# A three-part decoder layer on one core: prologue put in another order, first gate and up products ahead of the last head outputs, one bias product for two of three value blocks

## The reference, cut to what matters

```python
x = x + attn(layernorm(x))            # scores[0, -1] = scores[-1, 0] = -1e9, softmax over keys
x = x + xattn(layernorm(x), ctx, ctx, mask)
                                      # softmax(axis=1): over the 16 heads; V = ctx @ Wv + bv
x = x + ffn(layernorm(x))             # silu(gate) * up, then down
# ffn: inputs and weights in blocks of 16, block scales rounded to e4m3, values to the FP4 grid
```

## Time and profile before

| | |
|---|---|
| median of 3 runs | 611.21 us (610.62 to 612.62) |
| the profiled execution, its own time | 611.0 us |
| its span in the trace | 609.3 us |
| PE busy | 534.1 us, 88% |
| DVE busy | 511.8 us, 84% |
| ACT busy | 333.7 us, 55% |
| POOL busy | 354.6 us, 58% |
| mean granted TensorE clock | 0.975 of full |

### The profile page before, as it was taken

The page is one execution under the profiler, slowest core; times in us unless marked ns, Lnnn a source line. Parts: engine busy times, 40 slices in busy tenths (PEclk is TensorE's granted clock), DMA queues, the critical chain, the costliest instruction groups (busy, mean ns, idle before and its releaser), DMA issues. The chain is left out here.

```text
span 609.3 us, 14913 instructions
## 1 busy us (share of the span) xinstructions
PE 534.1 (88%) x6171; PEld 383.7 (63%) x6182; DVE 511.8 (84%) x658; ACT 333.7 (55%) x569; POOL 354.6 (58%) x292
## 2 busy tenths in 40 slices
PE   6799999997879999999999999998999676777855
PEld 6677777776557777767676667766776542443433
DVE  3687888897769878888898888888799989899997
ACT  3566766765445655555655575557555544444522
POOL 6411463333226677668768978877789764555540
PEclk9899999999989999999999999999999897899989
DMA  8910000000110011110110011101100000000001
GB/s 192 311 55 2 2 2 3 2 2 1 39 36 2 13 34 45 45 24 25 45 46 19 28 45 46 42 6 44 45 9 6 5 9 9 0 19 17 19 18 52
DMA packets 16645, 20.78 MB, mean 34 GB/s; under 512 B 2821, under 2 KB 14322, under 8 KB 16578
## 3 DMA queue, kind: packets, MB, share of 16 engines
q1 hardware_dynamic: 14658, 19.04, 10.5%
q10 hardware_dynamic: 1920, 0.79, 0.6%
HBM read 16.16 MB, written 1.84 MB: 30 GB/s over the span
## 5 line engine op out<-in xcount | busy, mean ns | idle before, releaser
L446 POOL TENSOR_TENSOR work<-work,rden 125x1792 f32<-125x1792 f32 x48 | 172.2, 3587 | 3.8
L985 ACT ACTIVATE work<-scores 125x896 f32<-125x896 f32 x96 | 88.7, 981 | 95.9 <-PE scores L1360 94.5
L707 DVE TENSOR_REDUCE negmax<-scores 125x112 bf16<-125x1792 f32 x48 | 97.2, 2025 | 26.8 <-PE scores L1350 26.0
L715 DVE TENSOR_REDUCE den<-work 125x56 f32<-125x896 f32 x96 | 102.1, 1064 | 12.3 <-ACT work L985 11.9
L444 POOL TENSOR_TENSOR rden<-rden,stays 125x112 f32<-125x112 f32 x48 | 22.0, 458 | 81.1 <-DVE rden L720 81.0
L1360 PE MATMUL scores<-negmax,identb 125*125 125x448 bf16 x192 | 47.4, 370 | 16.5 <-DVE negmax L707 13.8
L620 DVE TENSOR_REDUCE a_mpad<-scores 112x8 bf16<-112x896 f32 x32 | 33.5, 1093 | 22.1 <-PE scores L1252 20.6
L1350 PE MATMUL scores<-qz,kT 32*125 32x224 f32 x768 | 49.8, 373 | 1.8 <-ACT work L985 1.1
L1386 PE MATMUL head_out<-work,v 125*32 125x112 f32 x1536 | 48.9, 267 | 0.2 <-POOL work L446 0.2
L1457 PE MATMUL wide<-ctxT,ck 128*128 128x375 f32 x128 | 48.2, 498 | 0.8 <-ACT ctxT L1005 0.8
L1468 PE MATMUL wide<-cv,ctxT 128*125 128x256 f32 x192 | 48.5, 378 | 0.0
(11 more groups left out here) (238 smaller groups left out, 1182.1 us busy)
## 6 DMA issues: line engine op xcount, KB each, us to landing
ctx_sb<-in_ctx SPq DMA_DIRECT2D x16, 375.0 KB
mask_sb<-in_mask_Bx1xSxS_if SPq DMA_DIRECT2D x16, 164.1 KB, 5.6
xsx<-in_x SPq DMA_DIRECT2D x4, 448.0 KB, 9.2
out_x<-ores SPq DMA_DIRECT2D x6, 256.0 KB, 2.1
a_raw_w<-in_L_ffn_gate_w SPq DMA_DIRECT2D x1, 1024.0 KB, 6.0
a_raw_w<-in_L_ffn_up_w SPq DMA_DIRECT2D x1, 1024.0 KB, 8.5
a_raw_w<-in_L_ffn_down_w SPq DMA_DIRECT2D x1, 1024.0 KB, 11.9
xt<-xsx SPq DMA_DIRECT2D x4, 112.0 KB, 2.2
```

The source lines that it names most:

```text
L446: pool.tensor_tensor(ex2[0:KP, kc], ex2[0:KP, kc], over, ALU.mult).then_inc(s["prob"], 1)
L707: dve.tensor_reduce(negmax[0:KP, :], scores[0:KP, :, 0:4 * TOK].rearrange("p j (h t) -> p t j h", h=4), AX.XY, ALU.max, negate=True).then_ ...
L715: link(dve.tensor_reduce(den[0:KP, kc, half], ex2[0:KP, kc, :, half, :].rearrange("p g t s -> p t g s"), AX.XY, ALU.add))
L985: act.activation(ex2[0:KP, kc, 4 * i:4 * i + 4].rearrange("p (j m) t s -> p j m s t", m=NE), scores[0:KP, 2 * i:2 * i + 2, 0:4 * TOK].rear ...
```

## The change

- **Loads.** SP issues the value weights second, and waits for the fourth attention weight (not the biases) before the feed-forward weights, each with a semaphore of its own. ACT issues the biases before the output weights, and also the bias `cbv`.
- **Tables.** POOL's twenty-two affine selects go; DVE makes the tables from the identity matrix in eight instructions (`mask_tables`).
- **First tiles.** The first three sequences are written out on PE, ACT and DVE: the rows of scores of sequence 0 come before the projections of sequence 1. The output weights are transposed into bank `head_out` and not `scores`. Statistics of group 1 come before the first row maxima, those of groups 2 and 3 behind them, each followed by its `shift`.
- **Value bias.** It moves from POOL at t = 8 to DVE at t = 2.
- **Passage to cross-attention.** On PE `score_rows` stands before the context input, `query` behind `maxima_T`, half of the first key product behind `maxima_T`. ACT normalises sequence 0 one iteration sooner and copies the context before the weight magnitude. In n = 0 PE subtracts the maximum after one value block instead of two, and DVE adds the last residual before the second block's maximum.
- **Passage to feed-forward.** On PE `gate(0, 0)` and `up(0, 0)` stand before the last sequence's head outputs of block 0, `gate(0, 1)` before the projection, `up(0, 1)` and `x_T(1)` before the head outputs of block 1. DVE takes the joint block maximum of x right behind the first `hidden`.
- **Bias product.** Blocks 0 and 1 of the values share a PSUM bank; one product of 512 columns (the 256 read twice) stands for two of 256.

```diff
@@ -317,19 +327,19 @@
...
-                sp.dma_start(raw[:, 0], whole(a_wq)).then_inc(ld_w[0], 16)
+                for n, w in ((0, a_wq), (2, a_wv)):
+                    sp.dma_start(raw[:, n], whole(w)).then_inc(ld_w[n], 16)
...
-                sp.wait_ge(ld_b, 48)
+                sp.wait_ge(ld_w[3], 16)
...
-                    if t == WFIRST + 2:
-                        value_bias()
...
@@ -586,7 +556,25 @@
...
+                def mask_tables():
+
+
+                    dve.wait_ge(a_s["made"], 2)
+                    link(dve.tensor_reduce(e_rows[:], identb[:].rearrange("p (j r) -> p r j", r=32)[:, 0:3, :], AX.X, ALU.add))
+                    link(dve.tensor_copy(aux[:], e_rows[:, 2:3].to_broadcast([P, TOK])))
...
@@ -604,6 +592,19 @@
...
+                def value_bias():
+
+                    dve.wait_ge(ld_v, 16)
+                    rest = cbv
+                    for n in range(3):
+                        link(dve.tensor_copy(bv_part[:], rest[:]))
+                        last = dve.tensor_copy(bv_parts[32 * n:32 * n + 1, :], bv_part[32 * n:32 * n + 1, :])
+                        if n < 2:
+                            link(last)
+                            link(dve.tensor_tensor(bv_rest[:], rest[:], bv_part[:], ALU.subtract))
+                            rest = bv_rest
+                    last.then_inc(s["bv_parts"], 1)
...
@@ -774,19 +775,24 @@
...
+                def joined_block_max(p):
                     if p == 0:
                         dve.wait_ge(s["wide_read"], 3 * B)
+                    b_amax = next(scale_parts(p))
+                    dve.wait_ge(s["x_norm"], 2 * joined[p] + 2)
+                    dve.tensor_reduce(b_amax[:, HBK:HBK + XBK], blocks(x_unit[:]), AX.X, ALU.max, apply_absolute_value=True)
...
@@ -860,17 +866,21 @@
...
-                for t in range(B + LAG):
+                statistics(1)
+                shift(1)
+                for t in range(1, B + LAG):
                     b = t - LAG
-                    if 0 <= b < B:
-                        row_max(b, 0)
-                        row_max(b, 1)
+                    if t != 2:
+                        row_max(rows_of(t), 0)
+                        row_max(rows_of(t), 1)
                     if 0 <= b - 1:
                         outputs(b - 1)
-                    if t < 3:
-                        statistics(t + 1)
-                    if 1 <= t < 4:
-                        shift(t)
+                    if t == 1:
+                        for g in (2, 3):
+                            statistics(g)
+                            shift(g)
+                    if t == 2:
+                        value_bias()
...
@@ -903,9 +913,10 @@
...
                         head_sum(now, 0, 0)
-                        key_max(now, 1)
                     if n == 0:
                         a_residual(B - 1)
+                    if now:
+                        key_max(now, 1)
...
@@ -933,6 +944,7 @@
...
                 hidden(0, 0)
+                joined_block_max(0)
                 residual(in_turn(B - 2))
                 hidden(0, 1)
...
-                for n, w in ((1, a_wk), (2, a_wv), (3, a_wo)):
-                    act.dma_start(raw[:, n], whole(w)).then_inc(ld_w[n], 16)
+                act.dma_start(raw[:, 1], whole(a_wk)).then_inc(ld_w[1], 16)
                 with nc.allow_non_contiguous_dma(reason="biases, one value per partition"):
                     for dst, bias in ((abq, a_bq), (abk, a_bk), (abv, a_bv)):
                         act.dma_start(dst[:], bias.rearrange("(a p) -> p a", p=P)).then_inc(ld_b, 16)
+                act.dma_start(raw[:, 3], whole(a_wo)).then_inc(ld_w[3], 16)
+                act.dma_start(cbv[:], c_bv.unsqueeze(0).to_broadcast([KP, D])).then_inc(ld_v, 16)
...
@@ -1099,62 +1112,87 @@
...
+                a_input_copy(0)
+                a_normal(1)
+                act.wait_ge(ld_b, 48)
+                act.wait_ge(a_s["bv_cols"], 1)
+                a_queries_keys(0)
+                a_values(0)
+                weight_copy(3, woT)
+                a_input_copy(1)
+                a_normal(2)
+                maxima_copy(0)
+                a_queries_keys(1)
+                a_values(1)
+                a_input_copy(2)
+                a_exp(0)
+                a_queries_keys(2)
+                a_values(2)
+                act.wait_ge(a_s["bv_ps"], 1)
+                act.copy(bv_row[:], a_y_ps).then_inc(a_s["bv_row"], 1)
+                a_normal(3)
+                for t in range(3, B + LAG):
                     b = t - LAG
...
                         input_copy(in_turn(0))
                         masks(in_turn(0))
-                        queries(in_turn(0))
...
+                        a_queries_keys(t)
+                        a_values(t)
+                    if t < B - 1:
                         a_normal(t + 1)
+                    if t == B:
+                        context_copy(in_turn(0))
...
-                    if t == B - 1:
-                        act.wait_ge(ld_c, 16 * 8)
+                    if t == B - 2:
+                        act.wait_ge(ld_c, 16 * 7)
                         normal(0)
-                    if t == B:
-                        context_copy(in_turn(0))
                     if t == B + 1:
...
@@ -1463,10 +1501,13 @@
...
                     out = wide[0:KP, kc // 2, (kc % 2) * D:(kc % 2 + 1) * D]
-                    pe.matmul(out, ones[0:65, :], bv_parts[0:65, :], start=True, stop=False)
+                    if kc != 1:
+                        both = wide[0:KP, 0] if kc == 0 else out
+                        pe.matmul(both, ones[0:65, :], bv_parts[0:65, :].unsqueeze(1).to_broadcast([65, 2 - kc // 2, D]),
+                                  start=True, stop=False, skip_group_check=True)
...
@@ -1534,35 +1575,59 @@
...
+                a_input_T(0)
+                first_projections(0)
+                pe.wait_ge(a_s["w_sb"], 3)
+                a_value(0)
+                a_weight_T(3)
+                pe.wait_ge(a_s["aux"], 1)
+                score_rows(0)
+                a_input_T(1)
+                first_projections(1)
+                maxima_T(0)
+                a_value(1)
+                score_columns(0)
+                a_input_T(2)
+                pe.wait_ge(a_s["mT"], 1)
+                bias_products()
+                first_projections(2)
+                a_value(2)
+                for t in range(3, B + LAG):
                     b = t - LAG
+                    score_rows(b)
                     if t == B:
-                        pe.wait_ge(ld_c, 16 * 8)
+                        pe.wait_ge(ld_c, 16 * 7)
                         input_T(in_turn(0))
                         mask_T(in_turn(0))
-                    if 0 <= b < B:
-                        if b == 0:
-                            pe.wait_ge(a_s["aux"], 1)
-                        score_rows(b)
-                    if 0 <= b - 1:
-                        a_head_outputs(b - 1)
+                    a_head_outputs(b - 1)
+                    if t == B + 1:
+                        key(in_turn(0), 0, 0)
+                    if t < B:
+                        a_input_T(t)
+                    if b == 1:
+                        pe.wait_ge(a_s["bv_row"], 1)
+                    maxima_T(b)
+                    if t < B:
+                        projected(t, 0, wqT)
                     if t == B:
                         query(in_turn(0))
                     if t == B + 1:
...
                         key(in_turn(0), 0, 1)
...
+                    score_columns(b)
+                    a_project(b - 1)
...
@@ -1591,8 +1647,13 @@
...
                         value(now, 0)
+                    if n == 0:
+                        less_max(now, 0)
+                    if now:
                         value(now, 1)
+                    if n > 0 and now:
                         less_max(now, 0)
+                    if now:
                         value(now, 2)
...
@@ -1627,21 +1688,23 @@
...
                         less_max(now, 2)
+                    if n == B - 1:
+                        gate(0, 0)
+                        up(0, 0)
+                    if now:
                         masked(now, 0)
                         head_outputs(now, 0, 0)
                         head_outputs(now, 0, 1)
                     if n == B - 1:
-                        gate(0, 0)
+                        gate(0, 1)
                     if old:
                         project(old)
                 final = in_turn(B - 1)
-                up(0, 0)
-                gate(0, 1)
+                up(0, 1)
+                x_T(1)
                 masked(final, 1)
                 head_outputs(final, 1, 0)
                 head_outputs(final, 1, 1)
-                up(0, 1)
-                x_T(1)
```

189 lines of the change are left out of this document (77 added, 112 removed).

## The result

The changed kernel took **604.44 us** in the median of five executions (601.83 to 606.66), the kernel before 610.62 beside it: a ratio of 0.990, 95% interval 0.986 to 0.994. Faster, as forecast, but by 6.2 us and not by 10.8, and 0.04 us outside the range. The executions of the changed kernel differ by 4.8 us, and the longer ones have the lower mean granted clock (0.972 in those of 606.45 and 606.66, 0.980 in that of 601.83). So there are two questions: which term was wrong in the profile, and what the other executions lose.

A forecast was written before the change was run, and what follows sets the result against it. Bounds: PE in self-attention, PE and DVE alternating in cross-attention, DVE in feed-forward. Gains 1.7 + 0.9 + 3.0 + 3.5 + 1.7 = 10.8 off the profiled 611.0 gave 600.2 us, range 597.8 to 604.4.

The forecast's parts named there:

- term 1: Start of self-attention: first scores 7.6 us sooner, but the second tile's maxima on DVE only 1.7 us sooner.
- rival (b): Start: PE's new 2.2 us wait for DVE brings the clock down, 0.8 plus 0.4 us, giving 601.4; chance 0.13.
- Term 2: Ninth self-attention tile: with the value bias off POOL, PE's 0.90 us wait through ACT goes; gain 0.9 us.
- Term 3: Passage to cross-attention: PE's waits of 1.98 (context input), 0.91 and 0.77 us shrink; gain 3.0 us, at least 2.
- Term 4: First cross-attention tile: residual before the second maximum on DVE ends PE's 2.64 us wait and half clock; gain 3.5 us.
- Rival (c): First cross-attention tile: POOL's product or ACT's copies set the next step, gain only 1, time 602.7; chance 0.10.
- Term 5: Passage to feed-forward: second up product 1.2 us sooner, joint maximum hidden for 0.6 less 0.1; gain 1.7 us.
- The bias product: Value products on PE: one of 512 columns for two of 256 saves at most 1.9 us; nothing taken.
- rival (e): Value products: the 512-column product reading 256 values twice is much slower, making the kernel slower, 613; chance 0.02.
- the shortfalls named for its high end: High end 604.4: Term 3 at 2.0, Term 4 at 2.6, Term 5 at 1.2, together with rival (b).

The follow-up runs named there:

- before_end: Kernel before with only the last stage of the change (first gate and up products earlier, joint block maximum between the hidden products): 609.48 us.
- the profile of 613.47: The kernel before, unedited, run again with a profile; half clock fell behind its wait for the first context input: 613.47 us.

## Why the prediction was right and wrong

**The step that failed: the start, term 1 with rival (b).** The order of events was right: each point on DVE came within 0.3 us of the forecast, and the difference to the profile was 1.84 against 1.7. What failed is what the prediction made of the clock around it, in two ways. First, "PE waits some 2.2 us for DVE" was entered without a price. The wait was 2.99, since PE came to it 0.75 earlier than forecast, and rival (b) had a chance of 0.13 and a price of 1.2 us; the clock fell in 7 of the 8 profiles that have this wait, at 1.6 us and once 3.1. The row on which (b)'s chance rested could not carry it: the 0.40 at 150.78 stands 5.5 us behind the wait of 1.98, and in the profile of 613.47, where the clock did fall behind that wait, the same product took 0.40 too (at 153.89). Second, the forecast took that one profile's start as the order's own time. It contained half clock (1.73 and 1.91 for projections of the form that the earlier trace rows show at 1.06 a tile earlier, a granted clock of 0.59 from 18 to 22), worth about 1.6 us, which two of the five profiles of before (with before_end) don't have. At the fourth tile's maxima these five stand at 48.1 in the mean (46.9 to 49.0), the nine of the changed order at 48.7 (47.2 to 50.5). The start, for which I gave 1.7 of gain, shows none; whether it loses the 0.6 is less sure, for so few profiles. It gains only where the wait is filled (47.26).

**Term 2**, the hiccup: 0.9 forecast, 2.89 - 1.84 = 1.05 measured. **Term 3**, the passage: 3.0 forecast, 5.37 - 2.89 = 2.48 measured; the 1.98 fell to 0.40 as said, but the wait before the last tile's scores grew from 0.89 to 1.09 and one of 0.48 for DVE's maxima is new. Missing from it was that the old wait sometimes took some 3 us more with it (in 1 of 5 profiles). **Term 4**: 3.5 forecast, 3.53 measured; against the other profiles of before it is 2.9 to 3.6. Its split was wrong, 0.7 of it being the subtraction's place. Rival (c) is out. **Term 5**: 1.7 forecast, 1.55 at equal clock. But the clock is not equal: in ten profiles of the changed order without filling, the passage took 33.09 in the mean, where the forecast implied 33.75 - 1.7 = 32.05. **The bias product**: 0 forecast, 0 measured; rival (e) is out.

**The end** was not in the sum at all: work that the change doesn't touch, shifted in time, lost 1.5 in half clock in 7 of 11 profiles. All five profiles of before (before_end among them) had 13.5 there. Why the shift matters is open.

**The median.** Laid stretch by stretch beside the forecast time, the profiles of the changed order (without filling at the place in question) are in the mean 1.4 us over it at the fourth tile's maxima (48.7 against 49.03 - 1.7), 0.5 on the way to the first maximum of cross-attention, 1.0 at the passage to the feed-forward part and 0.9 at the end: 3.8 of the 4.2 between 600.2 and 604.44. The other two profiles of the unedited kernel say the same: 604.79 is the first profile's 601.83 with 1.7 more at the start, 2.4 at the passage and 0.3 in the feed-forward part, less 1.5 at the end; 604.62 has 1.6 and 1.1 more at the start and the passage. Shown: where the clock falls, that idle products prevent it at the start and ahead of the feed-forward part, and what it costs there. That the profiled execution came within 1.6 us of the forecast is in part luck, since it is the one profile of eight that kept its clock at the start. Not settled: why before's longest executions reach 617 and 618, since no profile fell on one, and why the first comparison's before was that low.

**The range** ended at 604.4 because (b) was priced by one row instead of by the spread of executions. It was not worked out cleanly either: the shortfalls named for its high end, 1.2 + 1.0 + 0.9 + 0.5, add up to 603.8.
